# Perceiver cross-attention: transfers, norm and row statistics moved by a step, and the turn with keys at a stride of two, read back in two halves

## The reference

```python
def _L0_xattn_ref(x, context, w_kv, w_q, w_out1, w_out2, gamma):   # 16 heads of 64
    kv = context @ w_kv
    k, v = jnp.split(kv, 2, axis=-1)
    q = _split_heads(x @ w_q)
    ...
    dots = jnp.einsum('bhid,bhjd->bhij', q, k) * scale
    attn = jax.nn.softmax(dots, axis=-1)
    out = jnp.einsum('bhij,bhjd->bhid', attn, v)
    ...
def _L1_xattn_ref(x, latents, mask, Wq, Wkv, Wo, ...):             # 8 heads of 64
    xn = layernorm(x, ln_x_g, ln_x_b)          # x is the context here
    ln = layernorm(latents, ln_l_g, ln_l_b)    # latents: the 128 rows
    q = ln @ Wq
    kv_in = jnp.concatenate([xn, ln], axis=1)
    kv = kv_in @ Wkv
    ...                                        # masked softmax, values, Wo, layernorm
...
x = x + _L0_xattn_ref(_layernorm(x, axis=-1), ctx_1024, ...)
...
x = x + _L1_xattn_ref(ctx_1024, _layernorm(x, axis=-1), mask_BxS2_bk1, ...)
```

## Time and profile before

| What | Value |
|---|---|
| median of 3 runs (lowest to highest) | 2626.78 us (2623.25 to 2628.44) |
| profiled execution | 2626.45 us, span 2624.7 us |
| busy, PE / DVE / ACT / POOL | 2335.8 (89%) / 2007.8 (76%) / 1266.9 (48%) / 730.4 us (28%) |
| first stage, transposes (L756) | 224 of 1778 ns, 388.9 us |
| second stage, transposes (L756) | 112 of 1784 ns, 195.6 us |
| scatter and gather, first stage, median from issue to landing | 3.7 and 4.9 us |
| scatter and gather, second stage | 4.2 and 5.7 us |

### The profile page before, as it was taken

The page is one execution under the profiler, slowest core; times in us unless marked ns, Lnnn a source line. Parts: engine busy times, 40 slices in busy tenths (PEclk is TensorE's granted clock), DMA queues, the critical chain, the costliest instruction groups (busy, mean ns, idle before and its releaser), DMA issues. The chain is left out here.

```text
span 2624.7 us, 61865 instructions
## 1 busy us (share of the span) xinstructions
PE 2335.8 (89%) x23416; PEld 1876.9 (72%) x23416; DVE 2007.8 (76%) x4001; ACT 1266.9 (48%) x2509; POOL 730.4 (28%) x907
## 2 busy tenths in 40 slices
PE   8997999999999999977868989999667579999986
PEld 7886888888888888866757777777443247888873
DVE  7989899999999999975867888878652367666615
ACT  5544555555555555434645555555311264555553
POOL 1433143432443423330134545554000010010000
PEclk9999999999999999987989999999777689999996
DMA  6566556666666666556637777776377653444310
GB/s 258 204 225 220 211 204 235 238 238 241 220 217 225 239 239 227 201 186 224 218 120 267 265 263 262 259 257 241 134 306 289 252 183 118 128 142 128 88 48 23
DMA packets 179170, 540.96 MB, mean 206 GB/s; under 512 B 18012, under 2 KB 113456, under 8 KB 172736
## 3 DMA queue, kind: packets, MB, share of 16 engines
q1 hardware_dynamic: 176352, 528.52, 56.6%
q0 software_dynamic: 2304, 8.39, 0.9%
q10 hardware_dynamic: 224, 0.10, 0.0%
HBM read 356.76 MB, written 180.19 MB: 205 GB/s over the span
## 5 line engine op out<-in xcount | busy, mean ns | idle before, releaser
L511 PE MATMUL l0x_psum<-l0x_fast 128*128 128x512 f32 x1764 | 435.8, 399 | 1.5 <-DVE l0x_fast L713 1.0
L756 DVE STREAM_TRANSPOSE l0x_sbuf<-l0x_sbuf 128x896 f32<-128x896 f32 x224 | 388.9, 1778 | 0.6 <-issue 0.6
L511 PEld LDWEIGHTS l0x_psum<-l0x_fast 128*128 128x128 f32 x1764 | 323.1, 188 | 90.1 <-issue 22.6
L625 ACT ACTIVATE l0x_sbuf<-l0x_sbuf 128x896 f32<-128x896 f32 x224 | 234.7, 1048 | 281.3 <-DVE l0x_sbuf L736 281.3
L1808 DVE CUSTOM_DVE_ANT_0 l3x_sbuf<-l3x_psum,key_bias,l3x_sbuf 128x896 f32<-128x896 f32 x224 | 249.2, 1151 | 92.6 <-PE l3x_psum L1652 76.8
L1738 ACT ACTIVATE l3x_sbuf<-l3x_psum 128x512 f32<-128x512 f32 x392 | 221.4, 599 | 179.0 <-PE l3x_psum L1670 172.4
L491 PE MATMUL l0x_psum<-l0x_fast 128*128 128x448 f32 x1344 | 300.2, 372 | 0.0
L491 PEld LDWEIGHTS l0x_psum<-l0x_fast 128*128 128x128 f32 x1344 | 244.2, 188 | 25.0 <-DVE l0x_fast L719 0.3
L736 DVE CUSTOM_DVE_ANT_0 l0x_sbuf<-l0x_psum,l0x_sbuf 128x896 f32<-128x896 f32 x224 | 248.8, 1149 | 10.1 <-PE l0x_psum L526 10.1
L552 PE MATMUL l0x_psum<-l0x_sbuf 128*32 128x128 f32 x6272 | 204.6, 280 | 36.3 <-DVE l0x_sbuf L775 27.7
L552 PEld LDWEIGHTS l0x_psum<-l0x_sbuf 128*32 128x32 f32 x6272 | 173.5, 111 | 72.6 <-issue 61.2
(11 more groups left out here) (778 smaller groups left out, 4348.6 us busy)
## 6 DMA issues: line engine op xcount, KB each, us to landing
turns<-l0x_sbuf SPq DMA_DIRECT2D x112, 896.0 KB, 3.7
l0x_sbuf<-turns SPq DMA_DIRECT2D x112, 896.0 KB, 4.9
turns<-l1x_sbuf SPq DMA_DIRECT2D x56, 896.0 KB, 4.2
l1x_sbuf<-turns SPq DMA_DIRECT2D x56, 896.0 KB, 5.7
last_keys<-ctx_high SPq DMA_DIRECT2D x112, 224.0 KB, 3.5
ahead<-in_L_ffn_W SPq DMA_DIRECT2D x18, 1024.0 KB, 11.4
experts<-in_L_ffn_W SPq DMA_DIRECT2D x18, 1024.0 KB, 12.4
l0x_sbuf<-in_ctxT SPq DMA_DIRECT2D x14, 896.0 KB, 5.0
```

Of the source, the lines that this page charges most:

```text
L511: mm = pe.matmul(ps[:, :], x[:, c, t * T:(t + 1) * T], weights[w][:, c, :], start=(j == 0), stop=(j == len(products) - 1))
L625: act.activation(p, p, ACT.Exp, scale=-1.0, bias=self.negm[:, n % 2, 2 * pr + a:2 * pr + a + 1], accum_out=self.rs[:, m % self.RING, a:a + ...
L756: dve.transpose(self.blocks[:, j, :, a * CT:(a + 1) * CT, :].rearrange("p g t c -> p t g c"), self.p[:, a, :].rearrange("p (t r g) -> p t ...
```

## The change

Four things change in the two stages.

- **SyncE's order.** The gather stands directly behind its scatter, and the chunk's transfers behind the gather. The raw context of the chunk after next is issued at pr = 0 (behind gather(0)) instead of at pr = 1 (between scatter(1) and gather(1)); its wait for the low part is the same. Saves move from pr 2 and 3 to 1 and 2, the mask from 2 to 1, the rows of the next chunk to the last step of the chunk before. Mean and reciprocal deviation are issued apart, at pr 2 and 3, a chunk earlier than now.
- **The turn.** VectorE's transposes read keys at a stride of two, into two halves. The scatter still moves 896 KB; the gather becomes two transfers of 64 partitions and 448 KB each, one after the other on the same queue.
- **The norm of the second stage.** GpSimd does it at pr = 1 instead of pr = 2, first the two subtractions, then the two products, then the two gains.
- **The statistics of rows in the first stage.** VectorE does two of them in each step from pr = 4 on (the seventh alone), instead of one in each step from pr = 1 on.

```diff
...
         for m in range(self.P * NCH):
             n, pr = divmod(m, self.P)
             self.sp_scatter(sp, m)
+            self.sp_gather(sp, m)
             self.chunk_transfer(sp, n, pr)
-            self.sp_gather(sp, m)
             if m == 0 and self.side is None:
                 self.sp_out(sp)
             if m == self.P * NCH - 1 and self.side is not None:
...
     def chunk_transfer(self, eng, n, pr):
         s, ahead = self.s, n + 2
-        if pr == 0 and n > 0 and self.side is not None:
-            self.side.sp_rows(eng, n)
-        if pr == 0 and ahead < NCH and self.norm_dram is not None:
-            for c in range(DC):
-                eng.wait_ge(s.sem(f"scaled{c}"), ahead)
-            self.sp_norm(eng, ahead)
-        if pr == 1 and ahead < NCH:
+        if pr == 0 and ahead < NCH:
             eng.wait_ge(s.sem("c_low"), 2 * ahead)
             self.sp_raw(eng, ahead)
-        if pr == 2 and ahead < NCH and self.mask_dram is not None:
+        if pr in (1, 2) and ahead <= NCH and self.parts_dram is not None:
+            self.sp_save(eng, n + 1, pr - 1)
+        if pr == self.P - 1 and n + 1 < NCH and self.side is not None:
+            self.side.sp_rows(eng, n + 1)
+        if pr == 1 and ahead < NCH and self.mask_dram is not None:
             eng.wait_ge(s.sem("bias"), ahead)
             self.sp_mask(eng, ahead)
-        if pr in (2, 3) and ahead <= NCH and self.parts_dram is not None:
-            self.sp_save(eng, n + 1, pr - 2)
+        if self.norm_dram is not None:
+            if n == 0 and pr == 0:
+                self.sp_mean(eng, ahead)
+                self.sp_rstd(eng, ahead)
+            if pr == 2 and ahead + 1 < NCH:
+                self.sp_mean(eng, ahead + 1)
+            if pr == 3 and ahead + 1 < NCH:
+                self.sp_rstd(eng, ahead + 1)
 
     def sp_scatter(self, sp, m):
 
         s, j = self.s, m % 2
         sp.wait_ge(s.sem("blocks"), 2 * m + 2)
-        self.wait(sp, f"pT_in{j}", m // 2 * 16)
-        sp.dma_start(self.A["turns"][j], self.blocks[:, j, :, :, :].rearrange("p g t c -> p (g t c)")).then_inc(s.sem(f"blocks_out{j}"), 16)
+        self.wait(sp, f"pT_in{j}", m // 2 * 32)
+        sp.dma_start(self.A["turns"][j].rearrange("h p x -> p h x"),
+                     self.blocks[:, j, :, :, :].rearrange("p (h g) t c -> p h (g t c)", h=2)).then_inc(s.sem(f"blocks_out{j}"), 16)
 
     def sp_gather(self, sp, m):
 
         s, j = self.s, m % 2
         sp.wait_ge(s.sem(f"blocks_out{j}"), (m // 2 + 1) * 16)
         self.wait(sp, "values", m - 1)
-        sp.dma_start(self.pT[:, j, :, :, :].rearrange("p i t c -> p i (t c)"),
-                     self.A["turns"][j].rearrange("(i r) (g e) -> (r g) i e", i=4, g=4)).then_inc(s.sem(f"pT_in{j}"), 16)
+        for h in range(2):
+            sp.dma_start(self.pT[64 * h:64 * h + 64, j, :, :, :].rearrange("p i t c -> p i (t c)"),
+                         self.A["turns"][j, h].rearrange("(i r) (g e) -> (r g) i e", i=4, g=2)).then_inc(s.sem(f"pT_in{j}"), 16)
...
     def sp_raw(self, sp, n):
         sp.dma_start(self.raw[:, :, :], self.keysT_dram[:, :, n * CH:(n + 1) * CH]).then_inc(self.s.sem("raw_in"), 16)
 
-    def sp_norm(self, sp, n):
-        for name, dst, src in (("mean", self.mean, self.norm_dram[0]), ("rstd", self.rstd, self.norm_dram[1])):
-            sp.dma_start(dst[:, :], src[n * CH:(n + 1) * CH].partition_broadcast(128)).then_inc(self.s.sem(name + "_in"), 16)
+    def sp_mean(self, sp, n):
+        for c in range(DC):
+            sp.wait_ge(self.s.sem(f"centered{c}"), n)
+        sp.dma_start(self.mean[:, :], self.norm_dram[0][n * CH:(n + 1) * CH].partition_broadcast(128)).then_inc(self.s.sem("mean_in"), 16)
+
+    def sp_rstd(self, sp, n):
+        for c in range(DC):
+            sp.wait_ge(self.s.sem(f"scaled{c}"), n)
+        sp.dma_start(self.rstd[:, :], self.norm_dram[1][n * CH:(n + 1) * CH].partition_broadcast(128)).then_inc(self.s.sem("rstd_in"), 16)
...
         if self.short(m):
             pe.wait_ge(s.sem("turned"), m - self.P * NCH + 1)
         else:
-            pe.wait_ge(s.sem(f"pT_in{m % 2}"), (m // 2 + 1) * 16)
+            pe.wait_ge(s.sem(f"pT_in{m % 2}"), (m // 2 + 1) * 32)
...
         s, j = self.s, m % 2
         dve.wait_ge(s.sem(f"p{a}"), m + 1)
         self.wait(dve, f"blocks_out{j}", m // 2 * 16)
-        dve.transpose(self.blocks[:, j, :, a * CT:(a + 1) * CT, :].rearrange("p g t c -> p t g c"),
-                      self.p[:, a, :].rearrange("p (t r g) -> p t g r", t=CT, g=4)).then_inc(s.sem("blocks"), 1)
+        dve.transpose(self.blocks[:, j, :, a * CT:(a + 1) * CT, :].rearrange("p (h g) t c -> p t h g c", h=2),
+                      self.p[:, a, :].rearrange("p (t h r g) -> p t h g r", t=CT, h=2, g=2)).then_inc(s.sem("blocks"), 1)
...
             mine = slice(8 * g, 8 * g + 8)
             dve.tensor_tensor(self.acc[:, mine, :], self.acc[:, mine, :], add_cols(self.l[:, mine], self.HD), ALU.mult).then_inc(s.sem("attended"), 1)
 
-    def norm_part(self, eng, n, c):
-        s = self.s
+    def norm_center(self, eng, n, c):
+        s, part = self.s, self.raw[:, c, :]
         eng.wait_ge(s.sem("raw_in"), (n + 1) * 16)
         eng.wait_ge(s.sem("mean_in"), (n + 1) * 16)
+        eng.tensor_tensor(part, part, self.mean[:, :], ALU.subtract).then_inc(s.sem(f"centered{c}"), 1)
+
+    def norm_scale(self, eng, n, c):
+        s, part = self.s, self.raw[:, c, :]
         eng.wait_ge(s.sem("rstd_in"), (n + 1) * 16)
-        eng.wait_ge(s.sem("gain_in"), 32)
-        part = self.raw[:, c, :]
-        eng.tensor_tensor(part, part, self.mean[:, :], ALU.subtract).then_inc(s.sem(f"centered{c}"), 1)
         eng.wait_ge(s.sem(f"centered{c}"), n + 1)
         eng.tensor_tensor(part, part, self.rstd[:, :], ALU.mult).then_inc(s.sem(f"scaled{c}"), 1)
+
+    def norm_gain(self, eng, n, c):
+        s, part = self.s, self.raw[:, c, :]
+        eng.wait_ge(s.sem("gain_in"), 32)
         eng.wait_ge(s.sem(f"scaled{c}"), n + 1)
         eng.tensor_scalar(part, part, self.gain[:, 0, c:c + 1], self.gain[:, 1, c:c + 1], ALU.mult, ALU.add).then_inc(s.sem(f"normed{c}"), 1)
 
     def pool_norm(self, pool, n):
         for c in range(DC):
-            self.norm_part(pool, n, c)
+            self.norm_center(pool, n, c)
+        for c in range(DC):
+            self.norm_scale(pool, n, c)
+        for c in range(DC):
+            self.norm_gain(pool, n, c)
...
                     self.pool_context(pool, n + 1)
                 if n + 1 < self.N and self.mask_dram is not None:
                     self.pool_bias(pool, n + 1)
-            if pr == 2 and self.norm_dram is not None and n + 2 < NCH:
+            if pr == 1 and self.norm_dram is not None and n + 2 < NCH:
                 self.pool_norm(pool, n + 2)
...
                 self.dve_moments(dve, n, t)
         if pr == 4:
             self.dve_scales(dve, n)
-        if pr > 0:
-            self.dve_row(dve, n, pr - 1)
+        if pr >= 4:
+            for t in range(2 * pr - 8, min(2 * pr - 6, CT)):
+                self.dve_row(dve, n, t)
...
-        A["turns"] = nc.dram_tensor("turns", (2, 128, 2 * CH), F32, kind="Internal").ap()
+        A["turns"] = nc.dram_tensor("turns", (2, 2, 128, CH), F32, kind="Internal").ap()
```

More of the change, by code:

```diff
@@ L425, in sp_loads @@
             if self.norm_dram is not None:
-                self.sp_norm(sp, n)
+                self.sp_mean(sp, n)
+                self.sp_rstd(sp, n)
         if self.mask_dram is not None and n < NCH:
@@ L1352, in _ @@
             n0.moments(dve, link, x[:, :])
-            pa.norm_part(dve, 0, 0)
+            pa.norm_center(dve, 0, 0)
+            pa.norm_scale(dve, 0, 0)
+            pa.norm_gain(dve, 0, 0)
             n0.rescale(dve, link, lat[:, :], x[:, :])
             dve.sem_inc(s.sem("lat"), 1)
-            pa.norm_part(dve, 0, 1)
+            pa.norm_center(dve, 0, 1)
+            pa.norm_scale(dve, 0, 1)
+            pa.norm_gain(dve, 0, 1)
             dve.wait_ge(s.sem("latT_ps"), 1)
```

## The result

The changed kernel takes 2877.18 us (median of 5 runs, 2869.93 to 2886.94) where before takes 2623.25 (5 runs): 1.0966 times as long, 95% interval 1.0938 to 1.0993. Slower was forecast, at 2710 us and at most 2770; the loss of 254 us is three times the 84 of the sum. The profiled executions have spans of 2885.2 and 2624.7 us, 260.5 apart.

What follows compares the result with a forecast made beforehand. TensorE, busy 1133.8 of 1190.0 us in the first stage, was taken as the bound, so added waits are paid in full. First stage +58 − 23 = +35, second +49, together +84 on 2626.45: 2710 us, range 2640 to 2770.

Steps and rivals of the forecast that it cites:

- the mechanism and its place: At a chunk's second step SyncE's scatter waits for GpSimd's low part, so TensorE's values come late, 12 chunks in each stage.
- X = 5.4: At a chunk's second step, the scatter issued 0.65 us behind the raw transfer would take 5.4 us.
- My upper end: Highest time allowed for that scatter, 6.6 us, from a gather of as many bytes right behind a raw transfer.
- 58 + 78 − 29: Late values cost +58 us in the first stage and +78 in the second, where two replaced waits give back 29.
- the second half 0.37 behind the first: Of the two 64-partition gathers, the last lands 0.37 us after the whole would, one issue later.
- B: The gather halves are slow: each late gather ends 1.4 us later still, 24 times, +34, 2744 us; chance 0.17.
- the second half is hidden in the others: At steps where the gather isn't late, the second half costs nothing; without that cover, up to 1.8 us each.
- the −23 of the transposes: Transposes at 1.09 us instead of 1.78 shorten TensorE's waits for VectorE in the first stage, −23 us in all.
- the rate after a wait: TensorE's 56 values matmuls take 3.22 us after a wait of some length, 1.76 otherwise: 1.46 added per chunk.
- C: Not slower: the lag of two steps takes in the late scatter and gather; 2624 us, or about 2580; chance 0.15.
- X + Y: At a chunk's second step, scatter's time plus that of the gather behind it; below 8.4 us the kernel gets faster.
- D: VectorE's transposes don't get faster at a stride of two: +14, 2724 us; chance 0.08.

Runs made afterwards that it cites:

- the moves: The changed kernel with the turn of before (keys at a stride of four, one scatter, one gather of 128 partitions): 2801.58 us, ratio 1.067 against before.
- two small moves on GpSimd: Kernel of before with GpSimd's low part ahead of the factor of step 0 and the norm at second step instead of third: 2581.23 us, ratio 0.9846.

## Why the prediction was wrong

- **Right: the mechanism and its place.** SyncE holds the second scatter of a chunk for GpSimd's low part (12 and 12 waits), TensorE pays in full. Taking that wait out, and with it the raw context's place close ahead of the scatter, gave back 173 of 176 in the moves.
- **Wrong: the scatter's price, X = 5.4.** It was 7.5 to 9.2 in the moves, on the mean 8.1 in the first stage and 7.7 in the second, and 7.5 to 9.4 in the changed kernel. I took the row of a scatter beside other transfers; a scatter close behind a raw context lands only after it. My upper end was a gather that took 6.6 there, which is at the short end of 24 such gathers (6.6 to 8.2). In the moves alone the long waits were 6.2 and 7.8 instead of 3.4 and 5.1: 12 x (2.8 + 2.7) = 66 us more than summed. With that, 58 + 78 − 29 + 66 = 173, for 176 measured. Most of the 66 is the scatter, 12 x (2.7 + 2.3) = 60; the gathers behind it (6.0 for 5.3, 5.1 for 4.8) make 12, and the second halves, which the moves alone do not have, take off 9.
- **Wrong: the second half 0.37 behind the first.** The pair takes 7.0 and its first half 4.6, so the second lands 2.4 behind the first, over the 1.5 that was the sign of B. Rival B's mechanism held, but at all steps and not at 24: the sentence that the second half is hidden in the others failed, as it also slows the scatter behind it. I had weighed 224 KB transfers into 32 partitions against it; those rows were no test of this case. In the kernel they go to every fourth partition (`kst[j][b:128:4, ...]`), so over all 128, while the halves are partitions 0 to 63 and 64 to 127. The 64 partitions cost 74 us alone in the old order, and the turn 76 on top of the moves (2877 against 2802), where I had −14 (−23, and 24 x 0.37).
- **Short: the −23 of the transposes.** TensorE's waits for VectorE in the first stage fell by 16.6, to 11.1, where under 10 was the sign; the small ones went, but the long one of 9.7, of which most should have gone, still is 8.7.
- **Right: the transposes' own time**, 1.097 for 1.09, though 1.09 was a choice between bounds without a row of that stride; TensorE's waits behind ScalarE (15.8 less, about 16 taken); and the rate after a wait, 3.19 for 1.76.
- **Rivals.** C, not slower, fell with X + Y at 14.5 and 15.8 in the two chunks shown against the 8.4 it needed; D fell with the transposes. Saves, mask and statistics were put at nothing. That held for the first stage of the moves (5.7 us of waits once the low part is early) but not with the slow halves (the 27 us above); for the second stage it stays open.

## What to carry to other kernels

On one queue what stands directly ahead of a transfer is part of its price: take its time from a row with the same neighbour and direction, not from its own median. Before moving a transfer with a wait past another, ask whether the wait can be ended sooner: here two small moves on GpSimd gave 1.5%. When a transfer is cut in two, cut along what the partitions hold, not along the partitions.

## What the runs showed of the hardware

- Two transfers of 448 KB into 128 partitions cost as much as one of 896 KB (ratio 1.0007); into 64 partitions each, 2.8% of the whole kernel.
- A scatter 0.65 behind a raw context took 7.5 to 9.2 (median 7.7, 23 chunks of the moves), where alone it takes 3.5; a gather in the same place took 6.6 to 8.2 (median 6.8, 24 chunks of before), where alone it takes 4.8. The order of two neighbours on the queue, by itself, was worth 78 us.
- Two scatters with an outermost destination dimension of four took 14 us for what one does in 3.5, with 0.26 of the DMA engines' time used; that the dimension is the reason was not tried.
- VectorE's transposes take 1.097 us at a stride of two and 1.778 at four.
